# A quantising stage on one Trainium2 core: two passes a tile in place of three

## The reference

```python
im = relu(x) as a matrix of 256 rows (channels)
mn = mean(im, axis=1);  im = im - mn
p = clip(u.T @ im, -cv, cv)
dmax, dmin = max(p, axis=1), min(p, axis=1)
scale = 255 / (dmax - dmin)
q = round((p - dmin) * scale) / scale + dmin     # 256 levels a channel
p = u @ q
p = p - mean(p, axis=1) + mn
```

## Time and profile before

| | |
|---|---|
| median of 3 runs | 2022.3 us (2018.68 to 2025.76) |
| the profiled execution: its own time | 2026.12 us |
| the profiled execution: its span | 2024.1 us |
| stage one / two / three, about | 0 to 565 / 565 to 888 / 888 to 2024 us |
| PE busy | 1681.3 us, 83% of the span |
| DVE busy | 1607.6 us, 79% |
| ACT busy | 1495.5 us, 74% |
| DMA in the whole span | 438.60 MB, mean 217 GB/s |

### The profile page before, as it was taken

How to read it: one execution, slowest core, us unless ns; L and a number is a source line. 1 busy time by engine, 2 the same in 40 slices (tenths; PEclk the granted TensorE clock), 3 DMA queues, 4 the chain that set the end, 5 groups by cost and what they waited for, 6 DMA issues and landing times.

```text
span 2024.1 us, 39142 instructions
## 1 busy us (share of the span) xinstructions
PE 1681.3 (83%) x13394; PEld 1315.2 (65%) x13394; DVE 1607.6 (79%) x2719; ACT 1495.5 (74%) x2026; POOL 460.3 (23%) x135
## 2 busy tenths in 40 slices
PE   8999999999921000038999999999999999999998
PEld 8999999999921000025666666666666666666664
DVE  6888888888879888868777778787878777777874
ACT  6777777777777997646777777777777777777776
POOL 7888888888800000000000000000000000000000
PEclk9999999999965555569999999999999999999999
DMA  9999989989878999930242313232232313132414
GB/s 333 374 339 345 374 316 370 372 313 373 328 296 323 369 392 391 399 148 33 81 159 79 159 79 156 82 141 97 119 119 97 141 79 159 79 159 79 158 66 192
DMA packets 95806, 438.60 MB, mean 217 GB/s; under 512 B 8480, under 2 KB 9632, under 8 KB 80672
## 3 DMA queue, kind: packets, MB, share of 16 engines
q1 hardware_dynamic: 95776, 438.21, 57.1%
HBM read 219.82 MB, written 218.37 MB: 216 GB/s over the span
## 4 chain that ended last, share of the span: by engine, by line
PE 49%; DVE 5%; issue 1%; ACT 0%; DMA 0%; DVEq 0%
PE y_ps L867 15%; PE z_ps L817 14%; PE d_ps L847 14%; PE cov_ps L831 4%; DVE hl L992 2%; DVE g L978 1%; DVE gg L984 1%; PE ch_ps L875 1%; PE ch_ps L857 0%; DVE gg L986 0%; PE ch_ps L858 0%; DMA q<-q_scratch 0%; PE cov_ps L834 0%; ACT yo L926 0%; DVEq L1020 0%
## 5 line engine op out<-in xcount | busy, mean ns | idle before, releaser
L269 POOL TENSOR_TENSOR xl<-xs,xh 128x1568 fp32r<-128x1568 f32 x128 | 459.4, 3590 | 97.2 <-ACT xh L229 97.2
L926 ACT ACTIVATE yo<-y_ps,att_cy 128x512 f32<-128x512 f32 (+2 forms) x448 | 314.5, 724 | 137.7 <-PE y_ps L867 125.9
L898 ACT ACTIVATE h<-z_ps,sb_h 128x512 f32<-128x512 f32 (+2 forms) x448 | 277.5, 636 | 80.7 <-PE z_ps L817 71.1
L867 PE MATMUL y_ps<-qr,udh 128*128 128x512 f16 (+2 forms) x896 | 313.5, 353 | 2.3 <-ACT yo L926 1.8
L817 PE MATMUL z_ps<-qr,wh 128*128 128x512 f16 (+2 forms) x896 | 314.3, 354 | 1.2 <-DVE qr L945 1.2
L817 PE MATMUL z_ps<-qr,wl 128*128 128x512 f16 (+2 forms) x896 | 314.3, 354 | 0.0
L867 PE MATMUL y_ps<-qr,udl 128*128 128x512 f16 (+2 forms) x896 | 313.0, 352 | 0.0
L978 DVE SCALAR_TENSOR_TENSOR g<-d_ps,late 128x512 f32<-128x512 f32 (+1 forms) x224 | 141.9, 634 | 197.5 <-PE d_ps L847 193.6
L229 ACT ACTIVATE xh<-xs 128x1568 fp32r<-128x1568 f32 x128 | 194.2, 1517 | 139.4 <-PE pp L286 139.4
L847 PE MATMUL d_ps<-vh,hh 128*128 128x128 f16 (+1 forms) x1600 | 282.3, 220 | 10.3 <-DVE hl L992 10.3
L847 PE MATMUL d_ps<-vh,hl 128*128 128x128 f16 (+1 forms) x1600 | 281.0, 219 | 0.0
(11 more groups left out here) (164 smaller groups left out, 3011.4 us busy)
## 6 DMA issues: line engine op xcount, KB each, us to landing
xs<-in_x_dram SPq DMA_DIRECT2D x128, 784.0 KB, 6.8
out_dram<-yo SPq DMA_DIRECT2D x31, 3136.0 KB, 9.3
pt<-p_scratch SPq DMA_DIRECT2D x56, 1568.0 KB, 9.5
p_scratch<-po_low SPq DMA_DIRECT2D x56, 784.0 KB, 7.8
p_scratch<-late SPq DMA_DIRECT2D x56, 784.0 KB, 7.8
q<-q_scratch SPq DMA_DIRECT2D x32, 784.0 KB, 5.0
q_scratch<-qt SPq DMA_DIRECT2D x28, 784.0 KB, 11.3
q_scratch<-q_res SPq DMA_DIRECT2D x8, 392.0 KB, 8.0
```

Source lines behind the costliest of these rows:

```text
L269: nc.gpsimd.tensor_tensor(xl[:, k % 2], xs[:, k], xh[:, k % 2].bitcast(F32), ALU.subtract).then_inc(split_done, 1)
L867: last = nc.tensor.matmul(y_ps[:, m, 0:widths[c]], part[:, k, m * P:(m + 1) * P], qr[:, slot, k, columns(c)], start=k == 0 and part is udh ...
L898: nc.scalar.activation(h32[:, par, m, 0:w], z_ps[:, m, 0:w], ACT.Relu, bias=sb_h[:, m:m + 1]).then_inc(z_read, 1)
L926: nc.scalar.activation(yo[:, slot, m, columns(c)], y_ps[:, m, 0:widths[c]], ACT.Identity, scale=att_cy[:, m, 0:1], bias=att_cy[:, m, 1:2]) ...
```

## The change

Stage two now has two passes a tile. VectorE reads `pt`, subtracts the channel's minimum `lo`, multiplies by `qa` and writes an unsigned byte to `qt`; the conversion at the output rounds and keeps to 0 to 255. ScalarE then copies the bytes onto themselves and sums them to `qsum`. This holds for all four tiles of a pair and for the resident tiles. `qb` and the rounding constant go. Since the bytes are now 0 to 255 and not -128 to 127, stage three's conversion subtracts 128, and so does the mean. SP waits for VectorE's pass at even tiles and for ScalarE's sum at odd ones, and the half store of a resident tile stands behind the first sample's store instead of in front of tile 1's load.

```diff
-    q_dram = nc.dram_tensor("q_scratch", [N, P, K, M], I8, kind="Internal").ap()
+    q_dram = nc.dram_tensor("q_scratch", [N, P, K, M], U8, kind="Internal").ap()
...
@@ SyncE
-                        if t == 0:
-                            sp.wait_ge(q_by_act, n + 2)
-                        elif more or t % K == K - 1:
-                            sp.wait_ge(q_by_dve, (TILES - 1) * n + 2 * t)
+                        if t % K == K - 1:
+
+                            sp.wait_ge(summed, K * n + t + 1)
+                        elif more:
+                            sp.wait_ge(quantised, K * n + t + 1)
                         if more:
                             sp.dma_start(pt[:, t], p0_dram[n + 2 + t // K, t % K]).then_inc(p_loaded[t], 16)
-                        if resident is not None and t == 0:
-
-
-                            i, h = resident
-                            sp.dma_start(q_dram[i + NL, :, h], q_res[:, h]).then_inc(res_stored[h], 16)
                         if t % K == K - 1:
-
                             sp.dma_start(q_dram[n + t // K], qt[:, t // K]).then_inc(q_stored[t // K], 16)
+                            if resident is not None and t == K - 1:
+                                i, h = resident
+                                sp.dma_start(q_dram[i + NL, :, h], q_res[:, h]).then_inc(res_stored[h], 16)
...
@@ ScalarE
-                def scale_tile(i, t):
-                    act.wait_ge(p_loaded[t], 16 * (i + 1))
-                    nc.scalar.activation(pt[:, t], pt[:, t], ACT.Relu, scale=qa[:, t % K:t % K + 1],
-                                         bias=qb[:, t % K:t % K + 1]).then_inc(scaled_done, 1)
-
                 def resident_tile(i, h):
...
+                    act.wait_ge(res_quantised, K * i + h + 1)
+                    nc.scalar.activation(q_res[:, h], q_res[:, h], ACT.Copy,
+                                         accum_out=qsum[:, h, bass.ds(i + NL, 1)]).then_inc(res_summed, 1)
+
+                def two_samples(p):
+                    for t in range(TILES):
+                        act.wait_ge(quantised, TILES * p + t + 1)
+                        nc.scalar.activation(qt[:, t // K, t % K], qt[:, t // K, t % K], ACT.Copy,
+                                             accum_out=qsum[:, t % K, bass.ds(2 * p + t // K, 1)]
+                                             ).then_inc(summed, 1)
...
@@ VectorE
-                settle(nc.vector.tensor_tensor(qb[:], lo[:], qa[:], ALU.mult))
-                nc.vector.tensor_scalar(qb[:], qb[:], -1.0, None, ALU.mult).then_inc(scales_done, 1)
 
                 def two_samples(i):
                     for t in range(TILES):
-                        dve.wait_ge(scaled_done, TILES * i + t + 1)
-                        nc.vector.tensor_scalar(pt[:, t], pt[:, t], LEVELS, MAGIC, ALU.min,
-                                                ALU.add).then_inc(rounded, 1)
-                        if t == 0:
-                            continue
-                        dve.wait_ge(rounded, TILES * i + t + 1)
-                        if t != K + 1:
+                        dve.wait_ge(p_loaded[t], 16 * (i + 1))
+                        if t % K == 0:
                             wait_from(dve, q_stored[t // K], 16 * i)
-                        nc.vector.tensor_scalar(qt[:, t // K, t % K], pt[:, t], MAGIC + HALF, None, ALU.subtract,
-                                                ALU.add, accum_out=qsum[:, t % K, bass.ds(2 * i + t // K, 1)]
-                                                ).then_inc(q_by_dve, 2)
+                        nc.vector.tensor_scalar(qt[:, t // K, t % K], pt[:, t], lo[:, t % K:t % K + 1],
+                                                qa[:, t % K:t % K + 1], ALU.subtract, ALU.mult).then_inc(quantised, 1)
 
                 def resident_tile(i, h):
...
+                    wait_from(dve, res_stored[h], 16 * i)
+                    nc.vector.tensor_scalar(q_res[:, h:h + 1], p_res[:, bass.ds(i, 1), h], lo[:, h:h + 1],
+                                            qa[:, h:h + 1], ALU.subtract, ALU.mult).then_inc(res_quantised, 1)
...
@@ VectorE, stage three
                 def convert(a, c):
-                    nc.vector.tensor_copy(qr[:, a, :, columns(c)], q8[:, a, :, columns(c)]).then_inc(q_converted, 1)
+                    nc.vector.tensor_scalar(qr[:, a, :, columns(c)], q8[:, a, :, columns(c)], HALF, None,
+                                            ALU.subtract).then_inc(q_converted, 1)
```

More of the change, by code:

```diff
@@ L25 @@
 F16 = mybir.dt.float16
-I8 = mybir.dt.int8
+U8 = mybir.dt.uint8
 AX_X = mybir.AxisListType.X
@@ L34 @@
 HALF = 128.0
-MAGIC = 2.0 ** 23
 TOP = 2.0 ** 15
@@ L360, in layer_kernel @@
             pt = sb("pt", [P, TILES, M], stack=b)
-            qt = sb("qt", [P, 2, K, M], I8, stack=b)
-            q_res = sb("q_res", [P, K, M], I8, stack=b)
+            qt = sb("qt", [P, 2, K, M], U8, stack=b)
+            q_res = sb("q_res", [P, K, M], U8, stack=b)
             qa = sb("qa", [P, K], stack=b)
-            qb = sb("qb", [P, K], stack=b)
             lo = sb("lo", [P, K], stack=b)
@@ L483, in _ @@
                 nc.scalar.activation(wfc_t[:], wfc_ps[:], ACT.Copy)
-                act.wait_ge(scales_done, 1)
-                def scale_tile(i, t):
-                    act.wait_ge(p_loaded[t], 16 * (i + 1))
-                    nc.scalar.activation(pt[:, t], pt[:, t], ACT.Relu, scale=qa[:, t % K:t % K + 1],
-                                         bias=qb[:, t % K:t % K + 1]).then_inc(scaled_done, 1)
-                def resident_tile(i, h):
-                    tile = p_res[:, bass.ds(i, 1), h]
-                    nc.scalar.activation(tile, tile, ACT.Relu, scale=qa[:, h:h + 1],
-                                         bias=qb[:, h:h + 1]).then_inc(res_scaled, 1)
@@ L496, in two_samples @@
[L496 to L507, removed]
-                    nc.scalar.activation(qt[:, 0, 0], pt[:, 0], ACT.Copy, bias=-(MAGIC + HALF),
-                                         accum_out=qsum[:, 0, bass.ds(2 * p, 1)]).then_inc(q_by_act, 2)
-                    scale_tile(p, 2)
-                    scale_tile(p, 3)
+                def resident_tile(i, h):
+                    act.wait_ge(res_quantised, K * i + h + 1)
+                    nc.scalar.activation(q_res[:, h], q_res[:, h], ACT.Copy,
+                                         accum_out=qsum[:, h, bass.ds(i + NL, 1)]).then_inc(res_summed, 1)
@@ L515, in round_of_pairs @@
                         resident_tile(i, h)
-                        two_samples(2 * i + h + 1, (i, h))
+                        two_samples(2 * i + h + 1)
                 two_samples(0)
@@ L521, in _ @@
                 resident_tile(0, 0)
-                two_samples(1, (0, 0))
+                two_samples(1)
                 act.wait_ge(scaled_w, 1)
@@ L526, in _ @@
                 resident_tile(0, 1)
-                two_samples(2, (0, 1))
+                two_samples(2)
                 act.wait_ge(scaled_v, 1)
@@ L692, in cb @@
                 return sb(name, shape, dt, stack=c_)
-            q8 = cb("q8", [P, 2, K, M], I8)
+            q8 = cb("q8", [P, 2, K, M], U8)
             qr = cb("qr", [P, 2, K, M], F16)
@@ L939, in settle @@
                     dve.wait_ge(prepare_step, steps[0])
-                dve.wait_ge(q_by_act, 2 * PAIRS)
-                dve.wait_ge(q_by_dve, 2 * (TILES - 1) * PAIRS)
-                dve.wait_ge(res_done, K * RES)
+                dve.wait_ge(summed, TILES * PAIRS)
+                dve.wait_ge(res_summed, K * RES)
                 def convert(a, c):
-                    nc.vector.tensor_copy(qr[:, a, :, columns(c)], q8[:, a, :, columns(c)]).then_inc(q_converted, 1)
+                    nc.vector.tensor_scalar(qr[:, a, :, columns(c)], q8[:, a, :, columns(c)], HALF, None,
+                                            ALU.subtract).then_inc(q_converted, 1)
                 settle(nc.vector.tensor_reduce(mq, qsum[:], AX_X, ALU.add))
-                nc.vector.tensor_scalar(mq, mq, 1.0 / (N * M), None, ALU.mult).then_inc(mean_q, 1)
+                nc.vector.tensor_scalar(mq, mq, 1.0 / (N * M), HALF, ALU.mult, ALU.subtract).then_inc(mean_q, 1)
                 nc.vector.memset(gg[:], 1.0)
```

10 lines of the change are left out of this document (3 added, 7 removed).

## The result

The changed kernel takes 2007.12 us, the median of five executions (2002.28 to 2008.71); the kernel before, in five beside them, 2022.3 (2018.68 to 2026.03). The ratio of the means is 0.9916, with an interval of 0.9894 to 0.9938. The median lies within the range that was forecast, 6 us above its point. The ten executions lie between 2001.4 and 2012.4, with 2003 in the middle, and why they spread is part of what follows.

The account below looks back on a forecast made before the run. Stage two was taken as bound by a landed-store loop with late loads, stage three by the matrix engine; 20 us less overhead and 1 us less tail, 21 in all, gave 2001 us against the 2022.3 median, range 1992 to 2016.

Parts of the forecast that it names:

- The passes: Stage two: VectorE's new byte-writing pass 1.85 us (bounds 1.79 and 3.48), ScalarE's byte pass 2.8; stage three's convert unchanged at 686 ns.
- the conversion's rival: Stage three: the convert drops to one element a cycle, 50 us more, 2050 in all; chance 0.07.
- the matrix engine's waits: Stage three: a sign against the forecast, the matrix engine waiting for `qr` or `hl` by more than now.
- The patches are late loads: Stage two: patches of about 314 GB/s at unchanged DMA share, 1.8 us each, read as near-starvation from loads issued late.
- One patch for each of 14 pairs, all from the landed store's loop: Stage two before: store landing, passes and issues take 9.4 us, next landing 11.35; a 20.76 us loop with one 1.8 us patch.
- the 25 us: Stage two before: what remains of 42 us overhead after gaps (12.9) and first start and last landing (some 4).
- 19.25 us a pair, between 18.9 and 19.85: Stage two after: a pair's period, from the bytes' 18.9 to a still slow load's 19.85; a rest of 0.35 a pair.
- The gaps: Stage two's head: empty DMA queue around VectorE's weight work, 5, 1.7 and 1.3 us, together 8 where 12.9 stand.
- its sentence on the clock: Second stage at the 1.2 GHz level, third at 2.4; the matrix engine has no work in the second, before or after.
- Overhead and tail: Stage two: overhead above the bytes' time 22 us where 42 stand; landed store to third stage's first load 11.6, was 12.6.
- The rule against it: DMA transfers between HBM and SBUF: the skill's limit of about 358 GB/s, which the prediction said is not the limit here.
- The rival at 2015: Stage two: patches belong to the memory, so only gaps and tail count; 2015, between 2009 and 2019; chance 0.13.

Follow-up runs that it names:

- a_early: Changed kernel with loads of tiles 1 and 3 issued once VectorE has read the buffer, without waiting for ScalarE's sum: 1997.44 us, ratio 0.9865.
- a_best: Changed kernel with both the early loads of a_early and the moved weight work of a_weights: median 1989.52 us, ratio 0.9862.
- a_best2: a_best, with the last pair's stores waiting for VectorE's pass alone, ScalarE's sums there writing over the loaded tile: 1985.27 us, ratio 0.9819.
- a_pass2: Changed kernel with VectorE's quantising pass done twice for each of the 56 tiles of the loop: 2040.62 us, ratio 1.0093.
- a_again: The changed kernel without any edit, a second set of five executions against the kernel before: 2001.71 us, ratio 0.9885.
- a_weights: Changed kernel with VectorE's weight work moved behind pairs 2, 3 and 4, ScalarE's last absolute value behind pair 3: 1997.02 us, ratio 0.9859.

## Why the prediction was right, point by point

- *The passes*: 1.85, 2.8 and no change in the conversion were measured as 1.91, 2.81 and 686 ns. The byte-writing pass keeps the rate of the pass without an accumulator; the prediction read 0.06 us for one per-partition scalar from the earlier trace rows and added it once for two, and twice would have given 1.92; the conversion's rival and the matrix engine's waits are out: it lasts 1136.3 us, as before.
- *The patches are late loads*: right in the main. Issue earlier and they are gone behind 660 us, with the spread between executions (a_early, a_best, a_best2); lengthen the loop and they come in every sample (a_pass2). But a late issue makes a patch likely and not certain: at 5.1 us ahead loads flow in 3.8 us in one execution of the change and in 5.2 in another, and the slow load of the head is issued over 9 us ahead. What in the queue or the memory decides between them stays open. One trait of the late patches may help who looks: the GB/s begin to fall within a microsecond of that load's issue (issued at 828.05 in a_again, 433 GB/s in the microsecond before and 408, 376, 339 in the next three; issued at 842.51 before, where 843 to 844 us has 389), while by the landings the lost time falls on the load itself, 5 us later.
- *One patch for each of 14 pairs, all from the landed store's loop*: only partly. In the earlier trace rows the loop is shown for a late pair. By the landings in the trace of before, 13 loads beside the two behind the long gaps flow 4.6 to 7.0 us, together 22 us more than at 3.77 each, so the 25 us were there. The resident pairs 2 to 8 of the kernel before were held by ScalarE, busy 36.5 of the 40 us from 700 to 740, and a third slot doesn't help them. The change frees both, so the sum came out right by a reading that was half right.
- *19.25 us a pair, between 18.9 and 19.85*: 18.88 in the profiled execution, 20.5 in the late pairs of the one profiled in a_again, 0.65 above the upper bound. The engines' part of the loop is as computed: 8.4 us from the landed store to the next store's issue in both (8.5 forecast). The landing takes 10.45 us in the one, where 9.5 was forecast for a load that isn't starved and the bytes set the pace, and 11.97 in the other, more than the 11.35 taken from before. So the time above the bytes isn't a rest of 0.35 us spread over all pairs, as I took it, but a second way of running that an execution falls into or not. This is the term that was mis-sized: the profiled execution gained 23.8, 21 were forecast, and the median of the first set gained 15. The profile of before, from which I took 14 patches, was one of its upper group (2026.12); near 2018, where its lower group lies, some of them are probably missing, which I did not see from three times.
- *The gaps*: 8 us forecast, 7.1 measured, at 622, 631 and 655. The first one's 5 us are 3.5, the second's 1.7 are 2.0, and the last, put at 1.3, is 1.6.
- *The matrix engine in stage two*. Timeline of the changed kernel, VectorE's two weight pieces:

```profile
618.75 0.16 DVE L572 TENSOR_TENSOR small<-b_sb,shift_ps 128x2 f32<-128x2 f32 x1 [10.32 <-PE shift_ps L453]
...
639.09 0.16 DVE L608 SCALAR_TENSOR_TENSOR small<-shift_ps,small 128x1 f32<-128x1 f32 x1 [4.80 <-PE shift_ps L464]
```

VectorE stands 10.3 us for the matrix engine's small sums in the changed kernel, and everything queued behind it, the resident tile and tile 0, waits too. Only the last 5.3 us of them are the sums (613.43 to 618.75); before that ScalarE finishes the pair's byte sums (612.34) and the two absolute values. The prediction priced this rightly in its head (5.3 us of sums, 2.9 of VectorE's chain), and its sentence on the clock, that the matrix engine has no work in stage two, contradicts that and is wrong.
- *Overhead and tail*: from the first load's issue (565.04) to the landed store (852.40) 287.4 us, 19.4 over the bytes' 268, for 22 forecast; the tail 11.63 for 11.6.
- *The rule against it*: the Trainium skill's DMA: Bandwidth & Descriptors, section Bandwidth, has HBM bind at about 358 GB/s. Here 424 GB/s were held for 180 us (a_best), so the other figure of the section, 425 for one core, is the one that this kernel meets.
- *The rival at 2015*, only gaps and tail: the medians, 2007 and 2002, lie outside its range, and a_early, a_best2 and a_pass2 speak against its mechanism, as above.

## What to carry to other kernels

A DMA share of 0.99 says that transfers are in the queue, not that they run at full rate: put GB/s beside it over windows of a few microseconds, and where it dips at an unchanged share, look for the instruction that issued the next load late. Follow the loop from a store's landing over the passes and the waits of the queue's engine to the next store: where that loop is longer than the bytes need, microseconds on it count once a pair, as the doubled pass shows, although VectorE stood idle for 133 us of stage two. When a kernel has two ways of running, compare profiles of the same way: a_weights, profiled with the loop's patches, seemed to give 4 us, and by its quickest execution it may be twice that. And look at the spread between executions as well as at the median, with enough of them; four were too few to say that it had gone.

## What I had not expected of the hardware

How long a 1568 KB load flows goes with how far ahead it was issued, at nearly the same DMA share. These are the loads issued from 660 us on in all ten profiles:

| issued ahead of the landing before it | loads | flow over 4.3 us |
|---|---|---|
| under 3 us | 16 | 16 (4.3 to 7.9 us) |
| 3 to 4.5 us | 30 | 20 |
| 4.5 to 7 us | 113 | 19 |
| over 7 us | 208 | 2 |

The others flow in 3.6 to 4.3 us, most of them in 3.7 or 3.8. Between 4.5 and 7 us the same program can run whole stretches in one way or the other (pairs of 18.88 and of 20.5 us). An operation of VectorE with two per-partition scalars that reads fp32 and writes unsigned bytes runs at 1910 ns for 3136 elements, 0.12 us above the 1790 of the pass with immediates and float output, and far from the 3420 of the accumulating one, which read fp32 and wrote bytes as well.
